# One DMA transpose per head-unit for the high and the low halves of the attention probabilities

## What is computed

```
xn = layernorm(x)
q, k, v = xn @ W_Q + b_Q, xn @ W_K + b_K, xn @ W_V + b_V       # 16 heads of 128
scores = where(causal, q k^T / sqrt(128), -100000)
attn = softmax(scores)
s = sum over heads of (attn @ v) @ W_O + b_O
g = silu( (silu(xn gate_w^T * gate_s) * (xn up_w^T * up_s)) down_w^T * down_s )
out = x + s * g
```

## Times and profile before

| | |
|---|---|
| median of three runs | 1112.88 us (1110.94 to 1117.75) |
| the profiled execution | 1109.62 us, span 1107.7 us |
| PE busy | 1080.1 us, 98% of the span |
| DVE busy | 785.5 us, 71% |
| ACT busy | 678.3 us, 61% |
| granted clock of PE | 0.999 of full speed |
| DMA transposes L502 | 128, 3.9 to 9.3 us from issue to landing, median 4.3 |

### The profile page before, as it was taken

One profiled execution on the slowest core, in us unless ns is written; L12 is line 12 of the kernel. 1 busy time (PEld: TensorE's weight loads), 2 busy tenths in 40 slices (PEclk: granted clock), 3 DMA queues, 4 the chain that ended last, 5 costly groups with the idle time before them and its releaser, 6 DMA issues.

```text
span 1107.7 us, 19624 instructions
## 1 busy us (share of the span) xinstructions
PE 1080.1 (98%) x6876; PEld 650.1 (59%) x6876; DVE 785.5 (71%) x1936; ACT 678.3 (61%) x1627; POOL 79.5 (7%) x108
## 2 busy tenths in 40 slices
PE   6999999999999999999999999999999999999998
PEld 3434444445656666666666666666666666666664
DVE  7766767665767777777777777777766666766676
ACT  6744454545667666766676666666666666556562
POOL 1000000001200000000000000000000000124433
PEclk9999999999999999999999999999999999999999
DMA  7435656577667767876886778668656667769875
GB/s 270 140 76 152 183 148 191 160 226 216 140 164 208 191 149 210 218 189 164 222 229 161 194 194 217 161 176 228 175 129 167 137 141 178 194 173 199 240 193 164
DMA packets 311291, 201.27 MB, mean 182 GB/s; under 512 B 251296, under 2 KB 279968, under 8 KB 310176
## 3 DMA queue, kind: packets, MB, share of 16 engines
q1 hardware_dynamic: 290272, 174.92, 62.0%
q10 hardware_dynamic: 17568, 14.16, 4.1%
q0 software_dynamic: 3360, 11.01, 3.1%
HBM read 106.73 MB, written 31.46 MB: 125 GB/s over the span
## 4 chain that ended last, share of the span: by engine, by line
PE 84%; DVE 5%; DMA 4%; ACT 3%; SPq 2%; issue 1%; POOL 0%; DVEq 0%; ACTq 0%
PE bank L625 76%; PE bank L786 9%; DMA arena<-arena 2%; DMA split_qk<-w_out 1%; ACT arena L1076 1%; DMA split_vo<-w_out 1%; SPq L415 1%; DMA b_o_rows<-b_o_dram 1%; DVE w_out L1162 1%; DVE arena L1269 1%; DVE arena L1264 1%; ACT arena L981 1%; DMA w_in<-attn_w_dram 1%; DVE arena L1148 0%; DVE arena L1207 0%
## 5 line engine op out<-in xcount | busy, mean ns | idle before, releaser
L625 PE MATMUL bank<-XT,arena 128*128 128x256 f16 (+2 forms) x1872 | 316.4, 314 | 2.7 <-issue 2.6
L625 PE MATMUL bank<-arena 128*128 128x512 f16 (+1 forms) x1124 | 276.4, 379 | 5.2 <-DVE arena L1269 4.9
L625 PEld LDWEIGHTS bank<-XT,arena 128*128 128x128 f16 (+1 forms) x1872 | 179.3, 98 | 112.2 <-issue 5.6
L1076 ACT ACTIVATE arena<-bank,neg_max 128x512 f32<-128x512 f32 (+3 forms) x256 | 132.7, 525 | 138.1 <-DVE neg_max L1397 138.0
L625 PE MATMUL bank<-ST,arena 128*128 128x256 f16 x1536 | 199.4, 273 | 1.4 <-DVE arena L1359 0.7
L625 PE MATMUL bank<-arena,XT 128*128 128x512 f16 x768 | 195.0, 379 | 0.7 <-issue 0.7
L625 PEld LDWEIGHTS bank<-arena 128*128 128x128 f16 x1124 | 107.4, 98 | 128.0 <-issue 13.9
L625 PEld LDWEIGHTS bank<-ST,arena 128*128 128x128 f16 x1536 | 147.9, 98 | 50.1 <-ACT arena L1051 4.0
L1397 DVE CUSTOM_DVE_ANT_0 bank<-bank,mask 128x512 f32<-128x512 f32 (+3 forms) x256 | 118.5, 517 | 39.1 <-PE bank L625 39.1
L1414 DVE SCALAR_TENSOR_TENSOR arena<-arena,inv_sum 128x512 f16<-128x512 f32 (+3 forms) x256 | 126.9, 557 | 3.6 <-ACT arena L1090 1.5
L1090 ACT ACTIVATE arena<-arena,inv_sum 128x512 f16<-128x512 f32 (+3 forms) x256 | 122.1, 551 | 0.0
(11 more groups left out here) (103 smaller groups left out, 1131.0 us busy)
## 6 DMA issues: line engine op xcount, KB each, us to landing
arena<-split_qk SPq DMA_DIRECT2D x64, 896.0 KB, 5.2
w_in<-attn_w_dram SPq DMA_DIRECT2D x64, 256.0 KB, 3.9
arena<-split_vo SPq DMA_DIRECT2D x8, 1024.0 KB, 6.8
split_qk<-w_out SPq DMA_DIRECT2D x30, 256.0 KB, 3.2
split_qk<-w_out ACTq DMA_DIRECT2D x26, 256.0 KB, 3.8
arena<-ffn_w_dram SPq DMA_DIRECT2D x8, 768.0 KB, 4.6
arena<-x_dram SPq DMA_DIRECT2D x20, 256.0 KB, 4.2
split_vo<-w_out SPq DMA_DIRECT2D x20, 256.0 KB, 4.1
```

The lines of the kernel that those rows point to most:

```text
L625: mm = nc.tensor.matmul(out, stationary(a, k), moving(b, k), start=first and n == 0 and i == 0, stop=last and n == len(tiles) - 1 and i == ...
L1076: e = nc.scalar.activation(probs[:, at:at + width], SC[b_][:, col:col + width], ACT.Exp, bias=neg_max[:, i:i + 1], scale=-1.0, accum_out=r ...
```

## The change

The two transposes of a unit become one, of all 26 blocks, issued when both the high and the low halves are complete. There is one completion semaphore, `pt_ok`, in place of two. PE waits for it once, before the first of the 12 matmuls; ACT and DVE both wait for it before they write the next unit's halves.

```diff
@@ semaphores
-        pt_ok = [sem("pt_hi_ok"), sem("pt_lo_ok")]
+        pt_ok = sem("pt_ok")
@@ SP, transpose_probs(n)
-                for part, split in ((0, p_hi), (1, p_lo)):
-                    sp.wait_ge(split, TT * (n + 1))
-
-                    sp.dma_start_transpose(out=PT[part], in_=P_SPLIT[part].rearrange("p b k -> p (b k)")
-                                           ).then_inc(pt_ok[part], 16)
+                sp.wait_ge(p_hi, TT * (n + 1))
+                sp.wait_ge(p_lo, TT * (n + 1))
+                sp.dma_start_transpose(out=pt.rearrange("p (b q) -> p b q", q=P), in_=p_split).then_inc(pt_ok, 16)
@@ PE, weigh_v(u)
-                pe.wait_ge(pt_ok[0], 16 * (u + 1))
+                pe.wait_ge(pt_ok, 16 * (u + 1))
                 for j in range(TT):
                     part(0, 0, j, first=j == 0)
                     part(1, 0, j)
-                pe.wait_ge(pt_ok[1], 16 * (u + 1))
                 for j in range(TT):
                     mm = part(0, 1, j, last=j == TT - 1)
@@ PE, weigh_last_v()
-                pe.wait_ge(pt_ok[0], 16 * NU)
-                pe.wait_ge(pt_ok[1], 16 * NU)
+                pe.wait_ge(pt_ok, 16 * NU)
@@ ACT, split_probs(n, groups)
-                    act.wait_ge(pt_ok[0], 16 * n)
+                    act.wait_ge(pt_ok, 16 * n)
@@ DVE, split_probs(n, groups)
-                    dve.wait_ge(pt_ok[1], 16 * n)
+                    dve.wait_ge(pt_ok, 16 * n)
```

## The result

The changed kernel is slower by 1.3%: 1127.37 us in the median of four runs (1124.29 to 1131.56) against 1111.91 us for four runs of the kernel before (1110.26 to 1117.75). The ratio estimated from the runs is 1.0128, with a 95% interval of 1.0097 to 1.0158; the two medians alone give 1.0139, inside it. The loss is clear of noise. The profiled execution took 1124.29 us, its span is 1122.4 us; it was the fastest of the four.

The account below looks back on a forecast made before the run. PE, busy 98% of the span, bounds the kernel. Terms of 0.4, 1.5, 0.4, 0.3, 1.7, 1.3 and 1.3 sum to 6.9 us: 1116.5 for the profiled execution, 1119.8 for the median; range 1112.5 to 1129.5.

Parts of the forecast that it names:

- likeliest case: Whole kernel: the prediction's own forecast of +4 to +11 us, given a chance of 0.58.
- the region to which the prediction gave 0.18: Whole kernel: slower by over 1%, that is over 1124 us; chance 0.18.
- Step 1: SP's issue of the one transpose: 0.86 us after s, the issue of the old pair, as it waits for DVE.
- Step 2: Transfer of 26 blocks: lands 5.8 us after its issue, between bounds of 5.4 and 6.7.
- fast-engine rival: Transfer: one stream runs quicker than two, landing at 4.5 us; only units 57 and 58 pay, 0 to +4 us; chance 0.18.
- the one in which every unit is late: Regular units: the big transpose lands later than 7.3 us after issue, so each stalls; +65 us at 8.0; chance 0.09.
- Step 3: Regular units 5 to 56 and 59: 1.5 us to spare in place of 3.6; 0.4 us allowed for all.
- Step 4: Short first units: PE stalls 1.5 us in unit 0, 0.4 in unit 1, 0.3 in units 2 to 4 together.
- Step 5: Units 57 and 58, where POOL's own DMAs compete: 1.7 and 1.3 us more waiting on PE.
- Step 6: Units 60 and 61, with no value product: landing 0.65 us late in each, 1.3 us for both.
- Step 7: SP, ACT and DVE: one issue less per unit on SP, ACT's next split comes long after the landing; cost nothing.
- the other signs: Profile: landing 5.4 to 6.1 us after issue; 7 to 9 PE waits, some 8 us in total, longest near 2.6.

Follow-up runs that it names:

- late pair: Kernel before, still two transposes of 13 blocks, but both issued only after the low halves are complete; ratio 1.0045, median 1117.41 us.
- wait first: Kernel before, its two transposes untouched, but PE asks for both ahead of its first weighing matmul; ratio 1.0025, median 1114.90 us.
- four pieces: Changed kernel with its 26 blocks sent in four transposes of 7, 6, 7 and 6, one count; ratio 1.0217 against the kernel before, median 1135.75 us.

## Why the prediction came out as it did

The measured 1127.37 us lies in the stated range, and the direction was right. The likeliest case was +4 to +11 us; it came to +15.5 in the medians, in the region to which the prediction gave 0.18. That it is inside the range is luck. The upper end, 1129.5, was worked out for a landing of 6.7 us in every unit, and the landing was 5.8; by the prediction's own sum that gives 6.9 us. The rest came from two things that the sum did not hold: a landing in unit 57 that grew from 10.7 to 15.7, and the clock after a wait. The account of where PE would wait was right, and the price of the two worst places far too low.

- **Step 1, the issue at s + 0.86.** Right: 0.08 after DVE's last low block.
- **Step 2, the landing.** Right to the tenth: 1.2 + 4.6 = 5.8 in unit 34, the median over all 64 units 5.8. The issue took 3.9 us where the prediction said 3.0 to 3.5; nothing hung on it. The fast-engine rival is out, and so is the one in which every unit is late. The 261 GB/s that the Trainium skill states in "DMA: Bandwidth & Descriptors", section "Latency and other measured facts", were not reached here: 0.85 MB in 4.6 us are again 185 GB/s.
- **Step 3, regular units.** Right: no waits in units 5 to 56; they cost 0.3 of the 0.4 allowed. (In two of the other kernels unit 9 did wait, 0.61 and 0.62.)
- **Step 4, the short first units.** The wait of unit 0 was 2.46 where 1.5 was taken and 2.3 the bound, with a landing of 7.5, the same in all four kernels that merge unit 0. What the step lacked altogether is the clock: +1.5 us behind that wait. Units 1 to 4 waited 0.54 to 0.56 and lost nothing. They had waited 0.39 for DVE at the same place before, and after units 1 to 3 0.19 for ACT a few rows on; those waits are gone. The sum had 0.7 for them, since it counted from a start that held the 0.39 already.
- **Step 5, units 57 and 58. This is the term that was mis-sized.** It took the landing of unit 57 as fixed or moved by 0.86 and priced the wait at 1.7, at most 2.1, and 1.3 for unit 58, 3.0 together. They cost 8.2: unit 57 8.7, while unit 58, now clear of POOL's loads, landed at 5.8, waited for nothing and gave 0.45 back. The slow pair of before (10.7 us from the first issue to the second landing) was read as a price to be carried over. But it depends on when the loads come and on how the blocks are sent: as a later pair it took 11.9 and 11.4, as one instruction 15.7. The rule of the Trainium skill quoted there ("DMA: Bandwidth & Descriptors", "Rules for kernel authors"), to issue a DMA early and wait late, pointed the right way: the late pair and the wait first together cost 0.76%. The part that the single instruction adds in unit 57 is not of that kind.
- **Step 6, units 60 and 61.** Predicted 1.3, found 3.1 in the changed kernel (2.29 and 0.54 of waiting), and 1.5 where only those units were merged. The landing of 7.5 in unit 60 is not a fixed cost of the place: in the three other kernels that merge it, it was 5.7 to 5.8.
- **Step 7.** Right for ACT, DVE and SP. But a line of POOL's waits 7.0 us for the load that collided, which delays nothing on PE. The prediction had named such a wait, of a line other than L784 on DMA, as a sign of being wrong, and it came; it is the other side of the collision that step 5 missed. Of the other signs, the number of waits (8) and the landing were as said, their total (16.1 in place of some 8) and the longest (8.6 in place of 2.6) were not.

What stays open: why one transpose of 26 blocks suffers more beside POOL's loads than two of 13. That it does is measured in two executions of each kind, with the loads at the same distance from the issue (15.7 and 16.3 against 11.9 and 11.4), and its packets took longer; why they did was not isolated. The four pieces rest on one execution. The 7.5 us landings are open too. In units 0 and 60 the query and key load was issued 4.1 us after the transpose, but units 2 to 4 had it as early and landed at 5.8.

## What to carry to other kernels

A transfer that is covered in 56 units of 64 is priced by the other eight: list, unit by unit, the slack between its landing and its use, before splitting or joining it. Where one such transfer already lands late because another queue's traffic runs beside it, do not carry its delay over as a constant. Its distance to the undisturbed landing was 4.9 us here (10.7 against 5.8); the later issue made it 6, the later issue and the larger instruction together 9.9. And a wait on the engine that bounds the kernel may cost more than its length: two of the waits here were followed by a clock at half speed, 1.4 to 1.5 us more for each.

## What the runs showed of the hardware

- **A transpose beside DMAs issued by POOL.** Without them 26 blocks take 5.8 us in the median, with 225 GB/s moved in unit 34 while the engines are busy. Beside four 256 KB loads of POOL's the same took 15.7 and 16.3 us in one instruction, at 124 GB/s in the worst stretch of the first with the engines' share at 1.18, and 11.4 and 11.9 us in two. Removing the loads from that stretch brought it back to 5.8.
- **The clock after a wait of PE.** Where PE stood for 2.46, 2.47, 2.73, 2.85, 3.52, 4.36, 4.55, 8.58 and 9.26 us before the weighing matmuls, the twelve that followed took 2.6 to 3.4 us and not 1.79; the mean granted clock over them was 0.50 to 0.56, and 0.64 and 0.67 in the two shortest cases (2.71 us after a wait of 2.47, 2.57 us after one of 2.85). Where it stood for 2.17, 2.21 and 2.29 us they took 1.79.
- **Short waits can be free.** In units 1 to 4 a wait of 0.55 us on PE cost nothing in the changed kernel, since it replaced one on DVE at the same instruction (0.39) and one on ACT soon behind it (0.19).
